# The integers of v as int16 in their own place, turned into bf16 by GpSimd during the maximum of the dots

## The reference, cut to what matters

```python
def fq_floor(x):                       # power-of-two scale from the maximum of |x|
    s = _pot_scale(x)
    return clip(floor(x / s), -128., 127.) * s

qkv  = fq_floor(fq_floor(h) @ fq_round(w_qkv))      # 2048 tokens x 3072
q, k, v = split(qkv, 3)
dots = einsum('bhnd,bhmd->bhnm', q, k) * temp
attn = fq_floor(softmax(fq_floor(dots)))
out  = einsum('bhnm,bhmd->bhnd', attn, v)
```

## Time and profile before

| | us |
|---|---|
| median of 3 runs (lowest, highest) | 481.63 (481.36, 481.78) |
| the profiled execution | 479.8 |
| its span in the trace | 478.0 |
| DVE busy | 420.0 (88%) |
| ACT busy | 350.2 (73%) |
| PE busy | 233.2 (49%) |
| POOL busy | 149.9 (31%) |

### The profile page before, as it was taken

The page is one execution under the profiler, slowest core; times in us unless marked ns, Lnnn a source line. Parts: engine busy times, 40 slices in busy tenths (PEclk is TensorE's granted clock), DMA queues, the critical chain, the costliest instruction groups (busy, mean ns, idle before and its releaser), DMA issues.

```text
span 478.0 us, 6808 instructions
## 1 busy us (share of the span) xinstructions
PE 233.2 (49%) x1541; PEld 106.5 (22%) x1541; DVE 420.0 (88%) x1396; ACT 350.2 (73%) x789; POOL 149.9 (31%) x323
## 2 busy tenths in 40 slices
PE   0269973878677733122222222119997718116031
PEld 0228411323122210011001111003342616102031
DVE  5879897889899999999999999958986985977967
ACT  3678983879899955999999999954776745537133
POOL 2500002001000002888889888870000005520010
PEclk9969995999755555555555555558999775557557
DMA  7500000000344520788888888792001300000002
GB/s 268 145 0 2 0 0 2 22 22 24 132 176 176 191 95 23 163 187 187 187 197 188 182 188 187 165 211 46 2 2 44 106 1 1 0 1 0 0 0 89
DMA packets 84210, 43.16 MB, mean 90 GB/s; under 512 B 69064, under 2 KB 74456, under 8 KB 84059
## 3 DMA queue, kind: packets, MB, share of 16 engines
q1 hardware_dynamic: 82618, 42.69, 34.2%
q10 hardware_dynamic: 1568, 0.21, 0.3%
HBM read 7.75 MB, written 1.58 MB: 20 GB/s over the span
## 4 chain that ended last, share of the span: by engine, by line
DVE 53%; PE 21%; issue 16%; ACT 7%; DMA 1%; DVEq 1%; ACTq 0%
PE ps L475 20%; DVE mem L1308 12%; DVE mem L1055 6%; DVE mem L1213 4%; DVE d_max L1058 4%; DVE mem L1496 2%; DVE row_max L1308 2%; DVE m L1633 2%; DVE m L1634 2%; ACT mem L903 2%; ACT mem L933 1%; DVE r_now L1054 1%; DMA bkv<-in_L_xattn_bv 1%; DVE row_code L1054 1%; DVE neg_max L1054 1%
## 5 line engine op out<-in xcount | busy, mean ns | idle before, releaser
L475 PE MATMUL ps<-mem 64*128 64x256 bf16 (+5 forms) x1188 | 175.0, 355 | 131.7 <-DMA mem<-mem 87.4
L933 ACT ACTIVATE mem<-mem,neg_max 128x256 f32<-128x256 int16 x256 | 126.2, 494 | 13.2 <-DVE neg_max L1054 9.4
L475 PEld LDWEIGHTS ps<-mem 64*128 64x128 bf16 (+3 forms) x1188 | 72.2, 122 | 229.0 <-issue 126.7
L1308 DVE CUSTOM_DVE_ANT_0 mem<-ps,fold,c 128x256 int16<-128x256 f32 x256 | 111.3, 471 | 0.0
L433 POOL TENSOR_SCALAR mem<-mem,r_now 128x256 int16<-128x256 f32 x176 | 80.9, 478 | 80.9 <-DVE r_now L1054 80.8
L1213 DVE TENSOR_TENSOR mem<-mem 128x1024 bf16<-128x1024 bf16 x82 | 54.3, 688 | 6.2 <-ACT mem L873 4.0
L888 ACT ACTIVATE mem<-ps,c 128x1024 bf16<-128x1024 f32 x48 | 48.4, 1294 | 1.6 <-PE ps L475 1.6
L933 ACT ACTIVATION_READ_ACCUMULATOR mem<-mem,neg_max 128x1 f32 x256 | 47.7, 186 | 0.0
L903 ACT ACTIVATE mem<-ps,c 128x1024 int16<-128x1024 f32 x32 | 36.4, 1211 | 13.8 <-DVEq L1250 8.5
L433 POOL TENSOR_SCALAR bv_fine<-mem,r_now 128x256 int16<-128x256 f32 x80 | 36.8, 479 | 5.0 <-DVE r_now L1054 5.0
L1058 DVE TENSOR_REDUCE d_max<-ps 128x1 f32<-128x1024 f32 (+1 forms) x34 | 38.0, 1126 | 0.3 <-PE ps L475 0.3
(11 more groups left out here) (207 smaller groups left out, 380.4 us busy)
## 6 DMA issues: line engine op xcount, KB each, us to landing
mem<-mem SPq DMA_DIRECT2D x64, 256.0 KB, 2.4
mem<-in_L_attn_w_qkv SPq DMA_DIRECT2D x1, 1536.0 KB, 9.3
mem<-in_x SPq DMA_DIRECT2D x2, 512.0 KB, 5.0
mem<-in_x SPq DMA_DIRECT2D x1, 1024.0 KB, 5.5
out<-mem SPq DMA_DIRECT2D x4, 256.0 KB, 2.2
xattn_matrix<-mem SPq DMA_DIRECT2D x1, 512.0 KB
mem<-in_L_attn_w_out SPq DMA_DIRECT2D x1, 512.0 KB, 5.0
mem<-in_L_ffn_W SPq DMA_DIRECT2D x2, 256.0 KB, 4.6
```

What stands on the lines that cost most here:

```text
L475: return te.matmul(o_, l_, r_, start=start, stop=stop)
L933: ins = sc.activation(e_ring[:, u % 4, pos], y_ring[:, u % 4, pos], ACT.Exp, scale=scale_reg, bias=neg_max[:, u % 4, pos:pos + 1], accum_o ...
L1308: ins = ve.tensor_tensor_reduce(y_ring[:, slot, pos], ps[:, 2 * slot + pos // 2, (pos % 2) * N:(pos % 2 + 1) * N], shift, col("g_dots"), - ...
```

## The change

The 16 units of v (units 8 to 11 of each group) are no longer put into the ring code_i. ACT and DVE write their int16 to v_ints, which is the same memory as v_codes (both types have two bytes). DVE has no cast for them any more. POOL gets 16 tensor_scalar instructions of 128 x 1024 (times 1.0, plus 0.0), int16 in and bf16 out in the same place, after its last split of xbv and before its first fine_unit. The first waits until all conversions of the code pass are done. PE waits for these 16 before the product with v. The ring code_i now has six slots for ACT's units of q and k and two for DVE's, and SP waits for the casts of q and k alone.

```diff
--- before.py
+++ after.py
@@ -119,6 +119,7 @@
 
         t_fine = mem[:, 0:128 * KB].rearrange("p (b g j n) -> p b g j n", b=B, g=GROUPS, j=16)
         v_codes = at(128, [TILES, INNER], BF16)
+        v_ints = at(128, [TILES, INNER], I16)
 
         abs_t = at(160, [3, UNIT], BF16)
         run_max = at(168, [3, UNIT], BF16)
@@ -249,6 +250,9 @@
         QKV_UNITS = 12
         QKV_MAX_DVE = (3, 7, 11)
         QKV_CODE_DVE = (2, 5, 8, 11)
+        QK_ACT = [u for u in range(8) if u not in QKV_CODE_DVE]
+        QK_DVE = [u for u in range(8) if u in QKV_CODE_DVE]
+        CODE_RING = len(QK_ACT)
         DOT_UNITS = 8
         DOT_MAX_DVE = (3, 7)
         QKV_MAX_RING = 3
@@ -293,11 +297,10 @@
                 sp.dma_start(stage[:, slot], qk_g[:, grp]).then_inc(sem(f"staged_{phase}{slot}"), 16)
 
 
-            n_act, n_dve = QKV_UNITS - len(QKV_CODE_DVE), len(QKV_CODE_DVE)
             for s in range(STAGES):
 
-                sp.wait_ge(sem("cast_a"), (s + 1) * n_act + 4)
-                sp.wait_ge(sem("cast_v"), (s + 1) * n_dve)
+                sp.wait_ge(sem("cast_a"), (s + 1) * len(QK_ACT) + CODE_RING)
+                sp.wait_ge(sem("cast_v"), (s + 1) * len(QK_DVE))
                 stage_group("max", s, s)
             with sp.Fori(0, B * GROUPS // STAGES - 1) as it:
                 for s in range(STAGES):
@@ -417,6 +420,12 @@
                     link(pl.tensor_tensor(xbv_rest[:], rest[:], xbv_parts[:, k], ALU.subtract))
                     rest = xbv_rest
             ins.then_inc(sem("xbv_parts"), 1)
+
+            for t in range(TILES):
+                pool.wait_ge(sem("qkv_code_act"), (GROUPS + 1) * (QKV_UNITS - len(QKV_CODE_DVE)))
+                pool.wait_ge(sem("qkv_code_dve"), (GROUPS + 1) * len(QKV_CODE_DVE))
+                pl.tensor_scalar(v_codes[:, t], v_ints[:, t], 1.0, 0.0, ALU.mult, ALU.add)\
+                    .then_inc(sem("v_codes"), 1)
 
 
             pool.sem_inc(sem("fine"), 4)
@@ -692,8 +701,7 @@
             pe.wait_ge(sem("attn_scale"), 1)
 
 
-            pe.wait_ge(sem("cast_v"), GROUPS * len(QKV_CODE_DVE))
-            pe.wait_ge(sem("cast_a"), GROUPS * (QKV_UNITS - len(QKV_CODE_DVE)) + 4)
+            pe.wait_ge(sem("v_codes"), TILES)
             for grp in range(B * GROUPS):
                 b, g = grp // GROUPS, grp % GROUPS
                 nth = grp // 2
@@ -898,9 +906,10 @@
                 for k, u in enumerate(acts):
                     nth = gi * len(acts) + k
                     act.wait_ge(sem("qkv_code_unit"), gi * QKV_UNITS + u + 1)
-                    act.wait_ge(sem("cast_a"), nth + 1)
+                    if u < 8:
+                        act.wait_ge(sem("cast_a"), gi * len(QK_ACT) + QK_ACT.index(u) + 1)
                     s = 2 * (u % QKV_RING)
-                    sc.activation(code_i[:, k % 4], ps[:, s:s + 2].rearrange("p a n -> p (a n)"), ACT.Identity,
+                    sc.activation(code_i[:, QK_ACT.index(u)] if u < 8 else v_ints[:, 4 * gi + u - 8], ps[:, s:s + 2].rearrange("p a n -> p (a n)"), ACT.Identity,
                                   scale=col("g_qkv"), bias=col("floor")).then_inc(sem("qkv_code_act"), 1)
                     if nth == 18:
                         act.wait_ge(sem("xm_ps"), 2)
@@ -1247,24 +1256,20 @@
 
             acts, dves = split(QKV_UNITS, QKV_CODE_DVE)
             dve.sem_inc(sem("qkv_code_dve"), len(dves))
-            dve.sem_inc(sem("cast_a"), 4)
+            dve.sem_inc(sem("cast_a"), CODE_RING)
             qk_h = qk.rearrange("p (f b) g s n -> p f b g s n", f=2)
-            v_g = v_codes.rearrange("p (g k) n -> p g k n", k=4)
 
             def cast_unit(gi, u):
                 if u in dves:
                     k = dves.index(u)
                     dve.wait_ge(sem("qkv_code_dve"), (gi + 1) * len(dves) + k + 1)
-                    src = code_i[:, 4 + k]
+                    src = code_i[:, CODE_RING + QK_DVE.index(u)]
                 else:
                     k = acts.index(u)
                     dve.wait_ge(sem("qkv_code_act"), (gi + 1) * len(acts) + k + 1)
-                    src = code_i[:, k % 4]
-                if u < 8:
-                    jj, kind, half = u // 4, (u // 2) % 2, u % 2
-                    ins = ve.tensor_copy(qk_h[:, half, :, gi, 2 * kind + jj], src.rearrange("p (b n) -> p b n", n=N))
-                else:
-                    ins = ve.tensor_copy(v_g[:, gi, u - 8], src)
+                    src = code_i[:, QK_ACT.index(u)]
+                jj, kind, half = u // 4, (u // 2) % 2, u % 2
+                ins = ve.tensor_copy(qk_h[:, half, :, gi, 2 * kind + jj], src.rearrange("p (b n) -> p b n", n=N))
                 if u in acts:
                     ins.then_inc(sem("cast_a"), 1)
                 else:
@@ -1277,11 +1282,11 @@
                     if u in dves:
                         dve.wait_ge(sem("qkv_code_unit"), gi * QKV_UNITS + u + 1)
                         s = 2 * (u % QKV_RING)
-                        ts(code_i[:, 4 + dves.index(u)], ps[:, s:s + 2].rearrange("p a n -> p (a n)"),
+                        ts(code_i[:, CODE_RING + QK_DVE.index(u)] if u < 8 else v_ints[:, 4 * gi + u - 8],
+                           ps[:, s:s + 2].rearrange("p a n -> p (a n)"),
                            col("g_qkv"), FLOOR, ALU.mult, ALU.add).then_inc(sem("qkv_code_dve"), 1)
-                    if u:
+                    if 1 <= u <= 8:
                         cast_unit(gi, u - 1)
-                cast_unit(gi, QKV_UNITS - 1)
 
             dve.wait_ge(sem("run_max_zero"), 2)
```

## The result

| | before | changed |
|---|---|---|
| median of the runs, us | 481.5 (479.68 to 481.78, 4 runs) | 487.36 (486.83 to 487.56, 4 runs) |
| the profiled execution, us | 479.8 | 486.8 |
| its span, us | 478.0 | 485.1 |

The ratio is 1.0128, with a 95% interval of 1.0102 to 1.0155: slower by 5.9 us in the medians, where +8.4 and 490.0 were forecast; 487.4 lies in the range. The two traces differ by 7.1 us in the span. The profiled execution before was among the fastest of the kernel before, which took 479.68 to 482.78 us in all that were timed, so the traces show the mechanism and the medians the size.

What follows compares the result with a forecast made beforehand. ACT sets the pace in the maximum of the dots, with DVE nearly full; neither is full in the code pass. -0.7 + 9.1 = +8.4 us on the 481.63 us median gave 490.0 us, range 485.5 to 493.5.

Steps and rivals of the forecast that it cites:

- Part 1: In the code pass, DVE loses 16 casts; of 5.4 us only 0.7 was to come back, between 0 and -5.2.
- Both places: Code pass: DVE's conversion in group 1 starting earlier, 0.45 us, and its last unit's conversion no longer behind a cast, 0.25.
- Part 2: POOL's 16 casts of 1024 columns, run after the code pass: 1.09 us each, 17.5 us in all.
- Part 3: In the maximum of the dots, POOL's casts hold up DVE's folds: 10.2 us less 1.1 of slack, +9.1 us.
- a turn costs the cast's 1.09: In the maximum of the dots, POOL and DVE's folds alternate, each fold that meets a cast waiting its full 1.09 us.
- The count: In the maximum of the dots, two thirds of 14 casts, 9.3, stand in the way of DVE's folds.
- DVE's slack: In the maximum of the dots, DVE's 0.07 us wait per 3.01 us period absorbs 1.1 us of the loss.
- the signs given: POOL's casts from near 122 to 145-150 us; some nine folds of 1.7 us; dots maximum ends 8 to 9 later.
- (a): In the maximum of the dots, POOL goes only beside reductions and its casts cost nothing: 480.9 us; chance 0.10.
- (b): POOL keeps the way into SBUF through its 16 casts, delaying the first fold: +14.5 us, about 494.5; chance 0.05.
- (c): POOL's int16 cast takes 1.6 to 2.5 us and outlasts the reduction: 497 us or more; chance 0.05.
- (d): In the code pass, losing DVE's casts gives nothing as ACT is full: 490.7 us; chance within the forecast's 0.80.

Runs made afterwards that it cites:

- e3_memset: Changed kernel with each POOL cast replaced by a memset of the same size, which writes and reads nothing: 480.59 us, ratio 0.9987.
- e4_before_plus: Kernel before, plus 16 POOL instructions of the same shape (v_codes times 1.0 onto itself) in the maximum of the dots: 488.26 us, ratio 1.0144.
- e2_paced: Changed kernel with each POOL cast held by a semaphore wait to run beside a reduction, one per reduction: 480.46 us, ratio 0.9991.
- e1: Changed kernel without POOL's 16 casts; ACT and DVE write v's unrounded values as bf16 straight to v_codes: 480.93 us, ratio 0.9995.
- e5_pieces: Changed kernel with each POOL cast cut into four of 256 columns, 64 in all: 484.96 us, ratio 1.0087.
- e6_inpass_paced: Changed kernel with 12 of the 16 POOL casts moved into the code pass, the last four paced beside reductions: 484.62 us, ratio 1.0089.

## Why the prediction was right

**Part 1, -0.7 us: right in place, slightly large.** The traces show -0.54 (43.53 to 42.99). Both places are where they were said to be. In the trace after, these are ACT's wait in group 1 and DVE's last conversion:

```profile
99.57 2.30 ACT L912 ACTIVATE mem<-ps,c 128x1024 int16<-128x1024 f32 x2 [1.82 <-PE ps L484]
120.69 1.28 DVE L1064 TENSOR_SCALAR mem<-ps,c 128x1024 int16<-128x1024 f32 x1 [0.37 <-PE ps L484]
```

ACT waits 1.82 us where it waited 2.13, a gain of 0.31 for the 0.45 taken, and the conversion starts 0.04 us after PE's last matmul on the unit (119.47 + 1.18 = 120.65) where it was 0.25, a gain of 0.21. One thing in these 43 us moves by more than the change, TensorE's granted clock between 83 and 87 us, where PE has f32 products to do. It goes from 1.2 to 2.4 GHz within these 4 us, sooner or later. This line gives its mean for before, as a share of 2.4 GHz (the third number from the right):

```profile
83.00:87.00 4.00, 4.00 (x19) 1.96 (x18) 2.65 (x5) 2.50 (x3) 0.00 (x0) 0.90 0.00 0
```

It is 0.90 before, with the rise at 83.8 us, and 0.89 in the trace after, but 0.66 in e3_memset and 0.67 in e4_before_plus, with the rise near 85.7, and their code passes last 43.83 and 44.41 us, though e3 has the changed kernel's code pass and e4 that of before. At like clocks the difference is 0.54 and 0.58 us, at unlike ones it can vanish: e2_paced with 0.77 needed 43.49. That the small gain is not visible in the ratios of e1, e2 and e3 one by one (all just under 1) is no wonder.

**Part 2, 1.09 us per cast: high by 0.08.** It measured 1.04 to 1.05, and 1.01 from one to the next. The estimate of 1.54 us, from the 1.8 cycles that the prediction took from the Trainium skill's "GPSIMD Engine Reference" (§ 3.1 Elementwise — side-by-side cycle accounting), was the worse guide. Between 256 and 1024 columns it is (1.01 - 0.37) / 768 = 0.83 ns a column (e5_pieces), the rate of f32 in the earlier trace rows; what differs is the fixed part, 0.37 for 0.455 at 256 columns.

**Part 3, +9.1 us: the mechanism as put, three sizes off.** That a bf16 fold meets POOL as an f32 one does was inferred and is shown by e1, e2 and e3 together. That they take turns holds to the instruction. The step that was mis-sized is "a turn costs the cast's 1.09": it costs 0.84, since 0.17 us of a cast's distance do not keep a fold waiting. The earlier trace rows had this already: the DVE instruction ends 0.55 us after POOL's, where it takes 0.69 alone, so it does not stand until POOL's is quite over, as the prediction read it. The count was short the other way, 11 folds and not 9.3: with 1.01 against the reduction's 1.13 the next cast gets in before the fold asks, so that all three folds of a period stand (the one behind the reduction at 0.72). The stalls come to 0.5 + 7 x 0.84 + 3 x 0.72 = 8.5 us, for 10.2 in the sum. DVE's slack took 0.7 and not 1.1: 0.08 in each of the three long periods and 0.07 in each of five behind the last cast (2.94 us in place of 3.01, up to 158 us); then DVE had caught up with ACT, which I had ruled out, and from there ACT sets the pace as before. The lag of 2 us was not there to close, as ACT too had waited for the folds (6.6 us). 8.5 - 0.7 = 7.8, the measured 7.82. The turn was too dear and the count too low, so that these two errors took part of each other away; that is luck. Of the signs given, POOL's last cast ended at 142.65 and not at 145 to 150, and the long folds lasted 1.39 to 1.55 us and not 1.7.

**The rivals.** (a), that POOL goes only beside the reductions, did not happen by itself, but e2 brings it about, and its price of nothing was right: 480.5 for 480.9. (b), that POOL keeps the port through its run, would show one fold of 14 us; none lasts over 1.55. (c) falls with part 2. (d), that part 1 gives nothing, is nearer than thought, as it gives 0.5.

**What stays open.** The traces add up to +7.1 us, the medians to +5.9 (+6.2 against 481.21, the kernel before as it was run beside e1 to e4, and +6.4 against e1). The kernel before scatters from 479.7 to 482.8 us and the changed one, in four runs, by under 1 us. The traces of before and e4_before_plus, with the same code pass at 0.90 and 0.67 between 83 and 87 us, differ by 0.9 us in it (43.53 and 44.41), so the clock may make that much of the scatter; why the changed kernel shows less of it was not tried.

## What to carry to other kernels

Before moving work from VectorE to an idle GpSimd, list what VectorE runs at that time: beside instructions with two SBUF inputs, or its own casts from SBUF to SBUF, each GpSimd instruction that reads SBUF and meets one costs VectorE most of its own time (0.84 of 1.01 us here), and beside instructions that read PSUM alone it is free. If such work has to go there, tie each piece to a stretch in which VectorE reads PSUM, with a semaphore that is already counted; one wait turned +6 us into none. And what is taken from an engine that is busy but not full comes back only where another engine waits for it: 16 casts, 5.4 us of VectorE's time, gave 0.5.

## What the runs showed of the hardware beyond this

- A POOL memset of 128 x 1024 bf16 beside two-input folds costs them nothing (0.686 us each), a tensor_scalar of the same size 0.84 us per turn.
- In turns, a POOL instruction of 1024 columns costs a fold 0.84 us at 1.01 alone, one of 256 columns 0.2 at 0.37 alone: some 0.17 us of either is free. Cutting the casts in four lowered the loss from about 6 to 3.9 us with the same columns: the turns are counted per fold, and half of the pieces passed beside reductions.
- A DVE cast of int16 to bf16 with one SBUF input waits for a POOL instruction that reads SBUF in the same way, 1.07 to 1.11 us in place of 0.42 (e6_inpass_paced).
- The granted clock between 83 and 87 us took mean values from 0.63 to 0.90 of 2.4 GHz in executions of nearly the same program up to there, and the same code pass was up to 1 us longer at the low end (42.99 us at 0.89, 43.95 in e5_pieces at 0.63).
